# Four graph layers on one core: TensorE's semaphores in the edge passes come from a drain and no longer from a matmul

## The reference

```python
# layer 0: a softmax over the edges of each node, per feature
m = x[src] + edge_attr_64
ex = exp(m - segment_max(m, dst)[dst])
agg = segment_sum(m * ex / segment_sum(ex, dst)[dst], dst)
# layer 1: two GCN convolutions (sums over neighbours)
# layer 2: gated messages with a batch norm over all edges
total = batchnorm(concat(x[dst], x[src], edge_attr_128) @ fc_w.T + fc_b)
aggr = segment_sum(sigmoid(gate) * softplus(core), dst)
# layer 3, twice: mean, minimum and maximum over the edges of each node
h = concat(x[src], edge_attr_16 @ We + be) @ Wpre + bpre
agg = concat(segment_mean(h), segment_min(h), segment_max(h))
```

## Time and profile before

| | |
|---|---|
| time, median of three runs | 14850.82 us (14830.06 to 14877.83) |
| time of the profiled execution | 14705.55 us |
| its span, first to last instruction | 14703.8 us |
| mean granted TensorE clock (1 is 2.4 GHz) | 0.692 |
| busy, share of the span | PE 45%, weight loads 37%, DVE 39%, ACT 22%, POOL 47% |
| the four passes with a gather | 2980, 2630, 2930 and 2975 us |
| MSG, the pass without one | 890 us |

### The profile page before, as it was taken

The page is one execution under the profiler, slowest core; times in us unless marked ns, Lnnn a source line. Parts: engine busy times, 40 slices in busy tenths (PEclk is TensorE's granted clock), DMA queues, the critical chain, the costliest instruction groups (busy, mean ns, idle before and its releaser), DMA issues. The chain is left out here.

```text
span 14703.8 us, 137345 instructions
## 1 busy us (share of the span) xinstructions
PE 6641.3 (45%) x43115; PEld 5403.4 (37%) x43115; DVE 5762.8 (39%) x8056; ACT 3193.9 (22%) x4896; POOL 6960.9 (47%) x6971
## 2 busy tenths in 40 slices
PE   3555555547987555555533233333332333332332
PEld 2333333336886444444411122222222332222222
DVE  2334343359924333333477522222222322222224
ACT  1212222216700000000067211111111111111111
POOL 3445555425502555555544345554444455544453
PEclk8666767658987777777755566666666666666666
DMA  5434444423464555555555222222222122222222
GB/s 97 128 121 135 134 133 133 125 73 157 193 238 151 180 175 177 178 176 174 178 174 187 76 82 82 85 84 80 84 81 86 54 85 82 82 84 81 81 83 65
DMA packets 1298130, 1783.26 MB, mean 121 GB/s; under 512 B 618169, under 2 KB 793068, under 8 KB 1288346
## 3 DMA queue, kind: packets, MB, share of 16 engines
q1 hardware_dynamic: 815543, 882.53, 18.9%
q10 hardware_dynamic: 269696, 616.64, 11.1%
q0 software_dynamic: 212704, 281.43, 8.8%
HBM read 921.96 MB, written 857.87 MB: 121 GB/s over the span
## 5 line engine op out<-in xcount | busy, mean ns | idle before, releaser
L586 POOL DMA_INDIRECT arena<-table_d,idx_src x3136 | 2958.5, 943 | 3142.8 <-DVE idx_src L1239 2004.5
L755 PE MATMUL pn<-ident,work 128*128 128x128 f32 x7056 | 1431.2, 359 | 4686.0 <-DVE work L1284 3738.9
L755 PEld LDWEIGHTS pn<-ident,work 128*128 128x128 f32 x7056 | 1175.8, 216 | 4912.1 <-issue 2640.9
L1284 DVE TENSOR_TENSOR_SCAN work<-keep,work,pn 128x512 f32<-128x512 bf16 x588 | 752.8, 1280 | 5218.2 <-ACT neg L996 4022.6
L586 POOL DMA_INDIRECT arena<-in_x_dram,idx_src x1568 | 1491.8, 951 | 1561.8 <-DVE idx_src L1239 1100.5
L1004 ACT ACTIVATE arena<-pn 128x512 f32<-128x512 f32 x1764 | 926.2, 598 | 5125.0 <-remote 3418.4
L586 POOL DMA_INDIRECT arena<-tsrc_d,idx_src x1568 | 1479.6, 944 | 1126.8 <-DVE idx_src L1239 656.8
L731 PE MATMUL pn<-ident,arena 128*128 128x128 f32 x4704 | 1019.2, 301 | 56.7 <-issue 56.5
L731 PEld LDWEIGHTS pn<-ident,arena 128*128 128x128 f32 x4704 | 834.7, 221 | 51.3 <-issue 51.3
L720 PE MATMUL pn<-work,weT 128*128 128x512 f32 x784 | 597.4, 855 | 550.7 <-issue 279.1
L730 PE MATMUL pn<-work,wblk 128*128 128x128 f32 x3136 | 725.8, 319 | 103.3 <-issue 73.2
(11 more groups left out here) (339 smaller groups left out, 12170.4 us busy)
## 6 DMA issues: line engine op xcount, KB each, us to landing
runs_d<-arena ACTq DMA_DIRECT2D x588, 768.0 KB
adj_d<-feat SPq DMA_DIRECT2D x37, 3136.0 KB, 10.8
feat<-adj_d SPq DMA_DIRECT2D x37, 3136.0 KB, 11.0
seed_d<-nothing SPq DMA_DIRECT2D x392, 256.0 KB
arena<-seed_d SPq DMA_DIRECT2D x392, 256.0 KB
attr<-in_edge_attr_dram SPq DMA_DIRECT2D x392, 256.0 KB
feat<-total_d SPq DMA_DIRECT2D x196, 512.0 KB
keep<-keep_d SPq DMA_DIRECT2D x588, 128.0 KB
```

The costliest lines, as they stand in the source:

```text
L586: g.indirect_dma_start(out=to, out_offset=None, in_=table, in_offset=bass.IndirectOffsetOnAxis(ap=idx, axis=0))\
L755: last = nc.tensor.transpose(pt[:, k, j * P:(j + 1) * P], of[:, 1 + j:1 + BLK:J], ident[:, :])
L1284: return SCAN(res[:, s, k, 1:BLK + 1], mask, data, res[:, 1 - s, k, BLK:BLK + 1], ALU.mult if mul else ALU.add, ALU.add if mul else ALU.mi ...
```

## The change

At the end of six steps of TensorE in the edge passes a drain follows the group of matmuls, and the drain raises the step's semaphore. The last matmul of the group no longer raises it. The steps are `turn_features`, `columns`, `turn_seeds`, `turn_back`, `decays` and `degrees`. The node phases, the GCN passes and `spread_mask` of `MSG` stay as they were. No matmul, wait or buffer is added or taken away. The core of the diff, which repeats in each step:

```diff
@@ turn_features
-                            last = nc.tensor.transpose(pe_[:, h, j:BLK:J], attr[:, u % 2, (h * J + j) * P:(h * J + j + 1) * P], ident[:, :])
+                            nc.tensor.transpose(pe_[:, h, j:BLK:J], attr[:, u % 2, (h * J + j) * P:(h * J + j + 1) * P], ident[:, :])
...
-                last.then_inc(s_eT.sems[u], 1)
+                pe.drain().then_inc(s_eT.sems[u], 1)
@@ columns
-                last.then_inc(s_col.sems[u], 1)
+                pe.drain().then_inc(s_col.sems[u], 1)
@@ turn_seeds
-                last.then_inc(s_seT.sems[u], 1)
+                pe.drain().then_inc(s_seT.sems[u], 1)
@@ turn_back
-                last.then_inc(s_row.sems[u], 1)
+                pe.drain().then_inc(s_row.sems[u], 1)
@@ decays
-                mm(to, identb, neg[:, v, half], start=False, stop=True, skip_group_check=True).then_inc(s_dec.sems[u], 1)
+                mm(to, identb, neg[:, v, half], start=False, stop=True, skip_group_check=True)
+                pe.drain().then_inc(s_dec.sems[u], 1)
@@ degrees
-                last.then_inc(s_hus.sems[u], 1)
+                pe.drain().then_inc(s_hus.sems[u], 1)
```

More of the change, by code:

```diff
@@ L700, in turn_features @@
                         for j in range(J):
[L701 removed]
+                            nc.tensor.transpose(pe_[:, h, j:BLK:J], attr[:, u % 2, (h * J + j) * P:(h * J + j + 1) * P], ident[:, :])
                 else:
[L703 to L704 removed]
+                    nc.tensor.transpose(pe_[:, 0, 0:P], attr[:, u % 2, 0:P], ident[:, :])
+                pe.drain().then_inc(s_eT.sems[u], 1)
             def columns(p, i, u):
@@ L721, in columns @@
                         for j in range(J):
-                            last = mm(to[:, j:BLK:J], gat[:, u, j, h, :], ident[:, :],
-                                      start=False, stop=True, skip_group_check=True)
+                            mm(to[:, j:BLK:J], gat[:, u, j, h, :], ident[:, :],
+                               start=False, stop=True, skip_group_check=True)
                 else:
@@ L730, in columns @@
                             mm(to, wblk[:, PNA.index(p), j, :], eT[:, s, 0:P], start=True, stop=False, skip_group_check=True)
-                        last = mm(to, gat1[:, u, j * P:(j + 1) * P], ident[:, :],
-                                  start=(p in (GCN1, GCN2)), stop=True, skip_group_check=True)
-                last.then_inc(s_col.sems[u], 1)
+                        mm(to, gat1[:, u, j * P:(j + 1) * P], ident[:, :],
+                           start=(p in (GCN1, GCN2)), stop=True, skip_group_check=True)
+                pe.drain().then_inc(s_col.sems[u], 1)
             def turn_seeds(p, i, u):
@@ L742, in turn_seeds @@
                     for j in range(J):
-                        last = nc.tensor.transpose((pt[:, 0, :], ph[:, :])[h][:, j:BLK:J], seed[:, u, h, j, :], ident[:, :])
-                last.then_inc(s_seT.sems[u], 1)
+                        nc.tensor.transpose((pt[:, 0, :], ph[:, :])[h][:, j:BLK:J], seed[:, u, h, j, :], ident[:, :])
+                pe.drain().then_inc(s_seT.sems[u], 1)
             def turn_back(p, i, u):
@@ L754, in turn_back @@
                     for j in range(J):
-                        last = nc.tensor.transpose(pt[:, k, j * P:(j + 1) * P], of[:, 1 + j:1 + BLK:J], ident[:, :])
-                last.then_inc(s_row.sems[u], 1)
+                        nc.tensor.transpose(pt[:, k, j * P:(j + 1) * P], of[:, 1 + j:1 + BLK:J], ident[:, :])
+                pe.drain().then_inc(s_row.sems[u], 1)
             def decays(i, u):
@@ L771, in degrees @@
                 for n in range(2 * J):
-                    last = mm(ph[:, 0:NT], hots_lo[:, u % 2, :, n], hots_hi[:, u % 2, :, n],
-                              start=False, stop=False, skip_group_check=True)
-                last.then_inc(s_hus.sems[u], 1)
+                    mm(ph[:, 0:NT], hots_lo[:, u % 2, :, n], hots_hi[:, u % 2, :, n],
+                       start=False, stop=False, skip_group_check=True)
+                pe.drain().then_inc(s_hus.sems[u], 1)
             def spread_mask(i, u):
```

## The result

The changed kernel takes 15803.59 us (median; 15791.22 to 15808.75), the kernel before beside it 14864.33 us. The ratio is 1.0631, with a 95% interval of 1.0605 to 1.0658: slower by 939 us. The prediction was 15490.

The account below looks back on a forecast made before the run. Bound: a loop of gather run, held semaphores, release, scans, next run. PNA 274, STAT 245, SOFT 98 and MSG 20 sum to 637 us; on 14705.55 plus 145 that gives 15490 us, range 11350 to 16300.

Parts of the forecast that it names:

- The drain waits, the signal doesn't pass: During gather runs a drain waits until held completions leave, its semaphore comes no earlier, TensorE stands; chance 0.43 as summed.
- PNA, 1.4 us a pair, 274: Both PNA passes, 196 pairs: 0.7 us for two drains and a matmul, 0.7 for late columns; 274 us together.
- a quarter: Share of PNA pairs where turn_back comes only with the release and 16 column matmuls, 2.7 us, stand behind it.
- STAT, 2.5 us a pair, 245: Statistics pass, 98 pairs: 1 us (features alone) to 5 us (columns too) of work follows the release; 245 us.
- SOFT, 1.0 us a pair, 98: Softmax pass, 98 pairs: degrees and turn_back fall behind the release, 2.4 to 4.4 us, mostly covered by VectorE; 98 us.
- the case that the cover is gone: Softmax pass without VectorE's work covering the delayed degrees and turn_back: 4 us a pair.
- Own cost of a drain, 0.25 us: TensorE time lost per drain itself; 686 us for all 2744, mostly beside other work.
- the 1.4 us of the prediction: In a PNA1 pair, the time from GpSimd's start of a 16-gather run to the first of three ScalarE reader starts.
- The signal passing: Rival: a drain's semaphore passes held completions, GpSimd becomes the bound in the gathering passes; median 11400 us, chance 0.40.
- Broken runs: Rival: drains wait and gather runs shrink from 16 to 8; 2120 us more in PNA, 17000 us, chance 0.06.
- No change: Rival: all drains lie in time when TensorE stood anyway; 14850 us, chance 0.08.

Follow-up runs that it names:

- increments_kept: The changed kernel with all 2744 drains in place, but each increment back on its group's last matmul: 15809.1 us.
- late_start_drains: The changed kernel plus, in the softmax pass, a GpSimd write of 128 x 1024 unread indices before each odd block's gathers: 1.0527 of the kernel before.

## Why the prediction was right, point by point

The direction, the mechanism and the order of size held. 15490 was 314 us too low. The sum came as near as it did by errors that partly cancel: PNA was some 216 us too low and SOFT 220, STAT 160 too high.

*The drain waits, the signal doesn't pass.* Right. Drains last up to 18.1 us (turn_back) and 34.6 (columns), the last held signals still come 3.3 us behind a run's last gather, PNA runs stay 16 long. The Trainium skill's rule, page "PSUM — Partial Sum Buffer", section "Engine vs sequencer instructions", that a drain waits for an idle engine, is what the trace shows in a sharper form: matmuls that have ended but whose completions are held keep the engine from idle. `increments_kept` shows that this alone is the cost.

*PNA, 1.4 us a pair, 274.* Right mechanism, wrong size. It is 382 us on the second chip (1.95 a pair), some 490 on the first (2.5). Both parts of the term were too small. A pair whose columns start more than 3 us behind the last gather was put at 0.7 + 2.7 = 3.4 us. It costs 5.0 (changed kernel) and 4.7 (late_start_drains), by how much later than the 3.38 us of before the features' reader starts behind the last gather (whatever the first chip adds by itself is in the 5.0); the columns then run at the clock's lower level and take 3.8 us, not 2.7. Any other pair was put at 0.7 us and costs 1.9 and 1.3. The share of such late pairs, "a quarter", was 92 of 190 on the first chip and 36 of 190 on the second. turn_back's drain alone costs 183 us on the third chip and some 320 on the first (6569 - 6249), the rest comes with the columns' own drain. The features' drain, which I had put first, is next to nothing by itself.

*STAT, 2.5 us a pair, 245.* Over: +85 in the changed kernel, +112 and +136 in two others with all drains. It is made of two terms of opposite sign, turn_seeds' drain (+190) and columns' (-44 in one kernel, -85 in another). A drain that comes out cheaper than nothing I had not allowed for; why columns' drain helps, by which many of the runs of 16 become runs of 8, stays open; the pass is 45 us shorter with drains even where no index list is read.

*SOFT, 1.0 us a pair, 98.* Under: +318, 3.2 us a pair, near the 4 that I had given for the case that the cover is gone. What went is not shown: it may be VectorE's cover, as I thought, or turn_back's lead over the hold, which is 1.3 us less in the pairs above. That the parts cost 0 to 43 us and all together 318 was not in the sum. The parts with decays' drain ran on other chips than the whole, so how much of the 318 is the first chip's own is open too.

*Own cost of a drain, 0.25 us.* 0.40 where TensorE is the bound; elsewhere it hides.

*A reading.* In the earlier trace rows the first of the three copies starts 1.8 us into the run (10030.59 - 10028.76); the 1.4 us of the prediction is a misreading on which nothing rests.

*The rivals.* The signal passing is refuted. Broken runs were not seen in PNA; in STAT they were, 82 runs of 8 where the kernel before has one, and the pass still grew by only 85 us. No change is off by 939 us.

What stays open: what makes the softmax pass 318 us longer, a threshold, the chip or something else, for which the changed kernel and its parts would have to run on one chip; and the mechanism by which a gather with indices keeps TensorE's completions.

## What to carry to other kernels

Leave the increment on the matmul. What a drain costs is what stands behind it in its engine's queue and would have been of use earlier, so look for the work that ran ahead under a stall and that it would now hold back; here one kind of drain cost 414 us and another 33. And where a trace has long waits for "remote" while GpSimd gathers, don't move the signal: break the runs of gathers, or take work that needs no signal out from behind the wait; here that was worth 8 to 10%.

## What the runs showed of the hardware

- Completions of TensorE's matmuls come late while GpSimd issues gathers with an index list one after the other at 1.25 us. They leave slowly during the run (turn_back's second reader in a PNA pair of before starts 17.1 us into the run at the median, its transposes 4.1 us into it), and the last come 3.3 us behind the run's last gather. With plain DMAs by the same engine (0.54 us each) there is none of it.
- A drain on TensorE waits for these completions too, up to 18.1 us behind twelve transposes of 1.6 to 2.8 us; without gathers by index it ends after at most 2.8.
- Waiting in the middle of a block until four gathers have landed costs GpSimd some 1767 us in all and makes the kernel 1445 us faster.
- One chip ran the unchanged kernel in 14870 us, another in 14607, 1.8% apart. With the same drains in the PNA passes the first chip took 6726 and 6742 us for them and the second 6471, and the long drain of a pair lasted 13.7 and 13.9 us against 11.8 at the median.
